# A convolutional GRU scan: the new value's input products move into the next convolution

## The reference

```
gi = x_line @ wih.T ; gh = h @ whh.T         # each 3 x 128: r, z, n
r = sigmoid(ir + hr) ; z = sigmoid(iz + hz)
n = tanh(i_n + r * h_n)
ctx = (1 - z) * n + z * h                    # kept for the output
h   = tanh(conv1d(ctx, cw, 3 taps) + cb)     # along the line, state of the next step
```

## Time and profile before

| | |
|---|---|
| time of the profiled execution | 352.39 us |
| its span, first to last instruction | 350.7 us |
| TensorE busy, 2725 matmuls | 325.7 us (93%) |
| VectorE busy | 294.3 us (84%) |
| ScalarE busy | 252.3 us (72%) |
| GpSimd busy | 11.0 us (3%) |
| mean granted TensorE clock | 0.988 |

### The profile page before, as it was taken

One profiled execution on the slowest core, in us unless ns is written; L12 is line 12 of the kernel. 1 busy time (PEld: TensorE's weight loads), 2 busy tenths in 40 slices (PEclk: granted clock), 3 DMA queues, 4 the chain that ended last, 5 costly groups with the idle time before them and its releaser, 6 DMA issues.

```text
span 350.7 us, 7730 instructions
## 1 busy us (share of the span) xinstructions
PE 325.7 (93%) x2725; PEld 263.0 (75%) x2725; DVE 294.3 (84%) x781; ACT 252.3 (72%) x587; POOL 11.0 (3%) x24
## 2 busy tenths in 40 slices
PE   0596869999999999999999999999999999999994
PEld 0254648888888888888888888888888888874442
DVE  1868849999999999999998998998989898996332
ACT  4967938888888878787777777777777777767500
POOL 2630000000000000000000000000000000000000
PEclk9999889999999999999999999999999999999999
DMA  7900000000000000000000000000000000001654
GB/s 299 401 3 2 2 0 2 2 0 3 3 0 2 1 2 2 1 2 3 0 0 0 0 0 0 0 0 0 0 0 0 0 0 0 0 2 30 173 153 125
DMA packets 10211, 10.61 MB, mean 30 GB/s; under 512 B 464, under 2 KB 8784, under 8 KB 10192
## 3 DMA queue, kind: packets, MB, share of 16 engines
q1 hardware_dynamic: 10192, 10.36, 8.7%
HBM read 6.16 MB, written 4.19 MB: 30 GB/s over the span
## 4 chain that ended last, share of the span: by engine, by line
PE 87%; ACT 4%; DVE 4%; DMA 3%; SPq 1%; issue 1%; ACTq 0%; DVEq 0%
PE rz_bank L839 23%; PE conv_bank L839 17%; PE rz_bank L842 11%; PE n_bank L839 11%; PE conv_bank L842 8%; PE n_bank L842 6%; DMA x<-x_dram 3%; PE rz_bank L948 2%; PE n_bank L952 1%; PE n_bank L950 1%; PE rz_bank L952 1%; PE rz_bank L950 1%; PE n_bank L948 1%; PE rz_bank L813 1%; ACT rz L467 1%; DVE stats L574 1%
## 5 line engine op out<-in xcount | busy, mean ns | idle before, releaser
L839 PE MATMUL conv_bank<-ctx_store,w_parts 128*128 (+1 forms) x558 | 107.8, 274 | 1.9 <-ACT hval L484 1.0
L839 PE MATMUL rz_bank<-x_rows,w_parts 128*128 128x256 f16 (+1 forms) x384 | 79.0, 273 | 5.7 <-DVE x_rows L616 4.2
L839 PE MATMUL rz_bank<-h_parts,w_parts 128*128 128x256 f16 x372 | 77.4, 276 | 0.6 <-DVE w_parts L624 0.5
L479 ACT ACTIVATE nval<-npre 128x256 f32<-128x256 f32 x93 | 38.7, 416 | 51.7 <-DVE npre L707 51.5
L467 ACT ACTIVATE rz<-rz_bank,descale 128x512 f32<-128x512 f32 x96 | 65.9, 687 | 12.2 <-PE rz_bank L839 4.6
L842 PE MATMUL conv_bank<-ctx_store,w_parts 128*128 (+1 forms) x279 | 66.5, 274 | 0.0
L839 PEld LDWEIGHTS conv_bank<-ctx_store,w_parts 128*128 128x128 f16 x558 | 54.5, 98 | 15.4 <-issue 2.6
L695 DVE SCALAR_TENSOR_TENSOR npre<-n_bank,descale,rz 128x256 f32<-128x256 f32 x93 | 45.0, 484 | 20.7 <-ACT rz L467 19.5
L484 ACT ACTIVATE hval<-conv_bank,biases,descale 128x256 f32<-128x256 f32 x93 | 51.3, 552 | 4.6 <-PE conv_bank L839 4.6
L842 PE MATMUL rz_bank<-x_rows,w_parts 128*128 128x256 f16 (+1 forms) x192 | 52.3, 273 | 0.0
L839 PE MATMUL n_bank<-x_rows,w_parts 128*128 128x256 f16 (+1 forms) x192 | 47.6, 275 | 0.0
(11 more groups left out here) (90 smaller groups left out, 410.0 us busy)
## 6 DMA issues: line engine op xcount, KB each, us to landing
x<-x_dram SPq DMA_DIRECT2D x8, 512.0 KB, 8.4
out_dram<-x_rows SPq DMA_DIRECT2D x8, 512.0 KB, 3.2
ctx_store<-weights_dram SPq DMA_DIRECT2D x3, 576.0 KB, 5.0
ctx_store<-weights_dram SPq DMA_DIRECT2D x1, 192.0 KB, 12.1
biases<-biases_dram SPq DMA_DIRECT2D x1, 2.0 KB, 11.7
```

The source lines that it names most:

```text
L479: nc.scalar.activation(nval[k][:], npre[k][:], ACT.Tanh).then_inc(n_done[k], 1)
L839: last = nc.tensor.matmul(out, w_block(HI, k, n), parts(hi_or_lo), start=start, stop=stop and hi_or_lo == LO, skip_group_check=True)
```

## The change

The products of the new value from the input are taken out of `input_products` (now `input_gates`, the 6 matmuls of r and z) and are a function of their own, `new_products`. It runs one block after the item's `hidden_products`, between the HI and the LO halves of the convolution of the item before it. In between, the recurrent part (now in the first half of `n_bank[k]`) has been multiplied by r in place by VectorE, and the input products add to that. `tanh` then reads the accumulator with the scale, as it did for step 0 alone. `tanh_argument` and the tile `npre` are gone.

`edges` are now the four outer rows on either side, `strip` the four last columns. All of `FIRST_ROWS` is split ahead, and three pieces of the second ring come in the opening instead of the blocks (1, 1) and (1, 2). The remaining core of the images is normalised in the blocks (1, 1), (1, 2) and (2, 0). The last store is cut in two, and the weights of the combination are split one block later.

```diff
--- before.py
+++ after.py
@@ -71,16 +71,16 @@
 RINGS = H // 4
 FIRST_ROWS = [Cells((row, row + 1), (0, W)) for row in (0, H - 1, 1, H - 2)]
 FIRST_COLS = [Cells((2, H - 2), (col, col + 1)) for col in (W - 1, W - 2)]
-AHEAD_PIECES = FIRST_ROWS[0:3] + FIRST_COLS[0:1] + FIRST_ROWS[3:] + FIRST_COLS[1:]
+SECOND_RING = ring_pieces(1)
+AHEAD_PIECES = FIRST_ROWS + FIRST_COLS + SECOND_RING[0:3]
 
 
 def pieces_of_blocks():
 
-    first = ring_pieces(1)
-    found = {(1, 1): first[0:2], (1, 2): first[2:4], (2, 0): first[4:5], (2, 1): first[5:6]}
+    found = {(1, 1): SECOND_RING[3:4], (1, 2): SECOND_RING[4:5], (2, 0): SECOND_RING[5:6]}
     for i in range(2, RINGS):
         for n, cells in enumerate(ring_pieces(i)):
-            found.setdefault(divmod(DIRS * (2 * i - 2) + n, DIRS), []).append(cells)
+            found.setdefault(divmod(2 * DIRS * i - 5 + n, DIRS), []).append(cells)
     return found
 
 
@@ -96,7 +96,9 @@
 POOL_UNITS = ("in 0", "rec 0", "conv 0", "in 1")
 DVE_UNITS = ("conv 1", "rec 1", "in 2", "conv 2", "rec 2", "comb")
 UNITS = POOL_UNITS + DVE_UNITS
-COMB_BLOCK = UNROLLED - 1, 1
+COMB_BLOCK = UNROLLED - 1, 2
+CORE_ON_ACT = {(1, 1): (5,), (1, 2): (6,), (2, 0): (7,)}
+CORE_ON_DVE = {(1, 1): (0,), (1, 2): (1, 2), (2, 0): (3, 4)}
 
 
 def build(nc, x_d, w_d, bias_d, out_d):
...
@@ -290,13 +291,13 @@
 
 
         def edges(ap):
-            return ap.rearrange("p (g r) w -> p g (r w)", r=2)[:, 0:H // 2:H // 2 - 1, :]
+            return ap.rearrange("p (g r) w -> p g (r w)", r=4)[:, 0:H // 4:H // 4 - 1, :]
 
         def strip(ap):
-            return ap[:, 2:H - 2, W - 2:W]
+            return ap[:, 4:H - 4, W - 4:W]
 
         def core(ap):
-            return ap[:, 2:H - 2, 0:W - 2]
+            return ap[:, 4:H - 4, 0:W - 4]
 
         def piece(ap, part, cells):
 
...
@@ -469,14 +477,9 @@
 
             def new_value(k, s):
 
-                if is_first(s):
-
-                    act.wait_ge(n_ready[k], 1)
-                    nc.scalar.activation(nval[k][:], n_bank[k][:, 0:COLS], ACT.Tanh,
-                                         scale=gate_scale(k)).then_inc(n_done[k], 1)
-                else:
-                    act.wait_ge(npre_done[k], s)
-                    nc.scalar.activation(nval[k][:], npre[k][:], ACT.Tanh).then_inc(n_done[k], 1)
+                act.wait_ge(n_full[k], s + 1)
+                nc.scalar.activation(nval[k][:], n_bank[k][:, 0:COLS], ACT.Tanh,
+                                     scale=gate_scale(k)).then_inc(n_done[k], 1)
 
             def hidden(k, s):
 
@@ -498,8 +501,10 @@
             def steps(t, j):
                 now, nxt, before = lagged(t, j, 0), lagged(t, j, -1), lagged(t, j, 1)
                 if isinstance(t, int):
+                    for b in CORE_ON_ACT.get((t, j), ()):
+                        normalise(b, core)
                     for cells in SPLIT_IN_BLOCK.get((t, j), ()):
-                        x_hi(cells, 3)
+                        x_hi(cells, 2 if (t, j) <= max(CORE_ON_ACT) else 3)
                     if (t, j) == COMB_BLOCK:
                         weights_hi(UNITS.index("comb"))
                 if exists(now[1]):
@@ -523,28 +528,27 @@
                 for b in ACT_NORMED[0:2]:
                     normalise(b, strip)
                 context_hi(1, 0)
-                normalise(ACT_NORMED[2], strip)
                 hidden(0, 0)
                 hidden_hi(0, 0)
+                normalise(ACT_NORMED[2], strip)
                 x_hi(FIRST_COLS[0], 2)
                 weights_hi(UNITS.index("in 2"))
                 hidden(1, 0)
                 hidden_hi(1, 0)
                 gates(0, 1)
-                x_hi(FIRST_ROWS[3], 2)
                 x_hi(FIRST_COLS[1], 2)
                 gates(2, 0)
                 new_value(2, 0)
+                new_value(0, 1)
                 weights_hi(UNITS.index("conv 2"))
-                new_value(0, 1)
                 context_hi(2, 0)
-                normalise(ACT_NORMED[0], core)
                 gates(1, 1)
+                x_hi(SECOND_RING[0], 2)
                 context_hi(0, 1)
-                for b in ACT_NORMED[1:]:
-                    normalise(b, core)
+                x_hi(SECOND_RING[1], 2)
                 hidden(2, 0)
                 hidden_hi(2, 0)
+                x_hi(SECOND_RING[2], 2)
                 weights_hi(UNITS.index("rec 2"))
 
             opening()
...
@@ -691,9 +696,9 @@
             def reset_hidden(k, s):
 
                 dve.wait_ge(sig_done[k], s + 1)
-                dve.wait_ge(n_ready[k], s + 1)
-                nc.vector.scalar_tensor_tensor(npre[k][:], n_bank[k][:, COLS:2 * COLS], gate_scale(k),
-                                               rz[k][:, 0, :], ALU.mult, ALU.mult).then_inc(rh_done[k], 1)
+                dve.wait_ge(n_ready[k], s)
+                nc.vector.tensor_tensor(out=n_bank[k][:, 0:COLS], in0=n_bank[k][:, 0:COLS], in1=rz[k][:, 0, :],
+                                        op=ALU.mult).then_inc(rh_done[k], 1)
 
             def context_lo(k, s):
                 dve.wait_ge(ctx_hi_done[k], s + 1)
@@ -701,20 +706,15 @@
                     context_lines(k, s, LO), context[k][:].rearrange("p l b -> p (l b)"), ACT_SCALE,
                     context_lines(k, s, HI), ALU.mult, ALU.subtract).then_inc(ctx_lo_done[k], 1)
 
-            def tanh_argument(k, s):
-
-                dve.wait_ge(rh_done[k], s)
-                nc.vector.scalar_tensor_tensor(npre[k][:], n_bank[k][:, 0:COLS], gate_scale(k),
-                                               npre[k][:], ALU.mult, ALU.add).then_inc(npre_done[k], 1)
-
             def hidden_lo(k, s):
                 dve.wait_ge(h_hi_done[k], s + 1)
                 nc.vector.scalar_tensor_tensor(h_parts[k][:, LO, :], hval[k][:], ACT_SCALE,
                                                h_parts[k][:, HI, :], ALU.mult,
                                                ALU.subtract).then_inc(h_lo_done[k], 1)
 
-            def z_times_h(k):
-
+            def z_times_h(k, s):
+
+                dve.wait_ge(rh_done[k], s)
                 nc.vector.tensor_tensor(out=rz[k][:, 0, :], in0=rz[k][:, 1, :], in1=hval[k][:], op=ALU.mult)
 
             def steps(t, j):
@@ -727,18 +727,18 @@
                 if isinstance(t, int):
                     for cells in SPLIT_IN_BLOCK.get((t, j), ()):
                         x_lo(cells)
+                    for b in CORE_ON_DVE.get((t, j), ()):
+                        normalise(b, core)
                     if (t, j) == COMB_BLOCK:
                         weights_lo(UNITS.index("comb"))
                 if exists(nxt[1]):
                     reset_hidden(*nxt)
                 if exists(now[1]):
                     context_lo(*now)
-                if exists(nxt[1]):
-                    tanh_argument(*nxt)
                 if exists(before[1], STEPS - 2):
                     hidden_lo(*before)
                 if exists(nxt[1]):
-                    z_times_h(nxt[0])
+                    z_times_h(*nxt)
 
             def opening():
                 blend(0, 0)
...
@@ -883,16 +881,19 @@
                         last = passes(halves[gate], k, gate, x_parts, LO, stop=gate == 1)
                 if first:
                     last.then_inc(rz_ready[k], 1)
-                elif isinstance(s, int) and s == 1:
-
-                    pe.wait_ge(n_done[k], 1)
-                else:
-
-                    pe.wait_ge(npre_done[k], s - 1)
-                passes(lines(n_bank[k][:, 0:COLS]), k, 2, x_parts, HI, start=True)
-                last = passes(lines(n_bank[k][:, 0:COLS]), k, 2, x_parts, LO, stop=first)
-                if first:
-                    last.then_inc(n_ready[k], 1)
+
+            def new_products(k, s):
+
+                first = is_first(s)
+
+                def x_parts(part):
+                    return x_line(k, s, part)
+
+                ahead(pe, s, x_parts(HI), x_parts(LO))
+                if not first:
+                    pe.wait_ge(rh_done[k], s)
+                passes(lines(n_bank[k][:, 0:COLS]), k, 2, x_parts, HI, start=first)
+                passes(lines(n_bank[k][:, 0:COLS]), k, 2, x_parts, LO, stop=True).then_inc(n_full[k], 1)
 
             def hidden_products(k, s):
                 def parts(part):
@@ -906,11 +907,12 @@
                     last = passes(rz_bank[k][:, gate * COLS:(gate + 1) * COLS], k, GATES + gate, parts, LO,
                                   stop=gate == 1)
                 last.then_inc(rz_ready[k], 1)
-                passes(n_bank[k][:, COLS:2 * COLS], k, GATES + 2, parts, HI)
-                passes(n_bank[k][:, COLS:2 * COLS], k, GATES + 2, parts, LO, stop=True) \
+                pe.wait_ge(n_done[k], s)
+                passes(n_bank[k][:, 0:COLS], k, GATES + 2, parts, HI, start=True)
+                passes(n_bank[k][:, 0:COLS], k, GATES + 2, parts, LO, stop=True) \
                     .then_inc(n_ready[k], 1)
 
-            def convolution(k, s):
+            def convolution(k, s, between=None):
```

(53 more changed lines are left out.)

24 lines of the change are left out of this document (11 added, 13 removed).

## The result

The changed kernel takes 371.16 us (median of 4 runs, 371.06 to 371.28), the kernel before 352.16 (4 runs, 351.92 to 352.49): a ratio of 1.0539, 95% interval 1.0521 to 1.0557, 19.0 us slower. The forecast was 378.5 us with a range of 371 to 387.

A forecast was written before the change was run, and what follows sets the result against it. TensorE's 27 matmuls bound the loop, with the circle through the gates hardly slack. From 352.4 us, +25.3 at block 94 (opening -6.3, loop +31.6), tail +1.6 and store -0.8 gave 378.5 us, range 371 to 387.

The forecast's parts named there:

- The circle: Loop: gates' matmuls, sigmoid, context HI, next convolution; lengthened by three matmuls, period 3.27 to 3.32 us against 2.945.
- the handover: Loop, from context HI to the next convolution: 0.53 us with TensorE otherwise at work, 0.58 where it stood waiting.
- low end: Whole kernel: block 8 at 49.1, period 3.27, tail +0.4, store -1.4 give 371.5 us.
- D: Loop: a block costs only the three matmuls' 0.33 us, 374 us; within the forecast's range, 82% together with it.
- the tail's two parts: End: +1.6 us from the last input products waiting for the multiply, -0.8 from the last store cut in two.
- (a): Opening: direction 2's first products no longer wait for HI and LO behind the fourth edge row, done about 1.5 us earlier.
- (c): Opening: the 3.48 us wait that ends at 47.75 goes, since row 2 is split by then.
- (b): ScalarE's opening: three core normalisations leave and three ring pieces enter, -2.1 us up to the weights of "rec 2".
- The give-back: Opening: 0.9 us given back for stretches at half clock, putting block 8 at 50.0, 6.3 us earlier.
- A: Loop rival: the circle doesn't bind, the loop keeps 2.945 us and only the opening counts, 347 us; 3%.
- B: Loop rival: TensorE's pauses drop the clock; a quarter of the blocks at the 1.2 GHz level gives 430 us; 4%.
- C: Rival: the loop loses but the opening gains nothing, block 8 at 56.3, 385 us; 10%.

The follow-up runs named there:

- early: Changed kernel with the late products two matmuls into the block instead of six: 371.62 us, period 3.237 us.
- moved: Kernel before, with the new value's input products issued a block later, ahead of the recurrent ones, dependency unchanged: 378.04 us, ratio 1.0698.
- moved_0: Kernel before, with the new value's three input products a block later, all behind the gates' matmuls: 353.27 us, ratio 0.9994.
- moved_1: Kernel before, with the new value's input products a block later, one ahead of the gates' matmuls and two behind: 358.53 us, ratio 1.0159.
- reorder: Changed kernel with the convolution's LO matmuls behind the gates, late products behind the first tap, ScalarE's and VectorE's orders altered: 350.01 us, ratio 0.9909 to the kernel before.
- reorder_tail: reorder_unrolled, with the first direction's products of chunks 2 and 3 moved ahead of the last late products: 347.04 us, ratio 0.9832.
- pieces_only: Kernel before, with all of the change but the late products (pieces, edges, cores, opening order, store in two): 346.10 us, ratio 0.9797.
- wait_last: Changed kernel with the two waits ahead of the convolution exchanged, accumulator first, then context HI: 377.62 us, ratio 1.0694, period 3.313 us.
- reorder_unrolled: reorder with steps 15 to 28 written out too, same order: 348.25 us, ratio 0.9865.

## Why the prediction was right, and where its size was off

**The bound and the mechanism held.** The circle has hardly any slack, ScalarE's order was left alone, and three matmuls ahead of the gates cost what they take. "early" and "moved" leave no room for the late dependency, and moved_0 and moved_1 show the length place by place. "Reorder" shows the cure: the count binds again once the gates' last matmul is the 15th. Even so the late products gain nothing: "reorder_tail" takes 347.04 us beside the 346.10 of "pieces_only", and TensorE's count is the same in both.

**The mis-sized term is the handover.** "From context HI to the next convolution it is 0.53 where TensorE had other work until then, and 0.58 where it stood waiting." In the loop it is 0.475. The 0.58 came from a context wait that was an instruction of its own, as "wait_last" shows. The 0.53 was no lower bound: it held slack, since TensorE wasn't waiting, 0.05 us of it. With 0.475 the forecast's sum is 1.853 + 0.31 + 0.58 + 0.475 = 3.218, within 0.02 of the measured 3.237 and below the 3.27 at which it put its low end. The loss a block is 0.29, where the forecast had 0.375 and "at least 0.33", so the loop came out below the forecast and D alike, and the time nearer to D's 374. From block 8 to block 94 that is 6.7 us of the table's 7.4 us of error (7.1 at the loop's pace, less 0.47 for the longer first block); the opening gave 0.7, and the tail's two parts cancel. The time, 371.16, therefore fell to the very foot of the range, and below the low end worked out for the forecast itself (371.5). That the range holds it is luck: its foot was set at 371 and not at the 371.5 of the sum. A sum that uses a handover seen elsewhere needs a lower end than that row. A row of the kernel before would have given it, the convolution of block 9, which came 0.48 behind context HI (block 10's too):

```profile
58.87 0.43 ACT L490 ACTIVATE ctx_store<-context 128x272 f16<-128x272 f32 x1
...
59.35 0.28 PE L839 MATMUL conv_bank<-ctx_store,w_parts 128*128 128x256 f16 x1
```

**The opening** went by steps (a) to (c). Item 5's recurrent products started at 40.19 (40.1 forecast). That this number is so close is in part luck: the terms given add up to 43.11 - 1.5 - 2.1 + 0.3 = 39.8 with (a), and to 41.3 without. Measured, (a) gave 1.4 (ScalarE's sigmoid of item 2 at 33.13 for 34.51) and (b) 1.6 (5.57 us from there to the weights of "rec 2", for 7.13). Then followed block 6 at 42.24 (42.3), block 7 at 45.55 (45.7), block 8 at 49.30 (49.1 before the 0.9 given back). The give-back was not needed: the clock stayed at 1.00 up to 40 us and beyond where it was 0.83 and 0.80 in the earlier trace rows. Not foreseen were one more long block, 3.7 us, behind block 8, and the 0.32 us that the late products waited for the multiply at 46.70, behind two cores that VectorE normalised (45.14 to 46.31). The forecast gave the whole gain to the pieces; "pieces_only" has 6.2 us of it.

**The tail** was right in both parts (+1.4 for +1.6, -0.6 for -0.8). Its wait is the 0.92 us at 335.30, and reorder_tail took it out for 1.2 us.

**The rivals.** A is refuted by moved_1: the circle binds from the 16th place on. For B, the clock read 1.00 through 268 us with a pause in each block, and in "wait_last" through 275 us with pauses of 0.37 us in 3.31, the forecast's own. The swing that the Trainium skill describes for short idles between groups of matmuls ("TensorE: Matmul & The Clock Gate", "A second HAM failure mode: psum-queue depth-cycling") was not seen at either; no loop here has longer pauses. C is refuted by block 8 at 49.30.

Left open: why the block's second matmul comes 0.120 behind the first in the changed kernel and 0.108 in "wait_last", and why VectorE's multiply is late in the four longer blocks of "reorder_unrolled".

## What to carry to other kernels

Where an engine is busy all the time, look for a second bound right beneath it: follow one consumer in a fixed queue order back to what it waits for, and count what stands ahead of that on the busy engine. Work with the same count can then still cost its full length by moving ahead of a signal. A change made of two parts should be timed in halves: here one half gained 6.0 us of span and the other lost 24.9.

## What the runs showed of the hardware

- The order of the two waits ahead of the convolution matters here: the first in the program is carried by the weight load, the second is an instruction of its own (51 ns), and the handover takes 0.565 instead of 0.475 us when the one that is met last is the second.
- A multiply in place in PSUM on VectorE (128x256 fp32) takes 432 ns against 484 for the same read with a result in SBUF and two factors, and matmuls then add onto what it wrote.
- In the block of "reorder" in which VectorE's loop branches, its blend starts 0.82 us after tanh instead of 0.51, 0.3 us later.
